# Layer 0 message weighting on VectorE: one two-harmonic product with the harmonics in PSUM and one addition, instead of one product and four scalar passes

## The reference

```
xs_e, xv_e = x[src][:, :64], x[src][:, 64:].reshape(E, 32, 3)      # rows of the source nodes
es, ev = edge_feat[:, 0], edge_feat[:, 1:4]                        # the four harmonics of an edge
out_s = (xs_e*es @ W_ss / 8 + einsum('eud,ed,uo->eo', xv_e, ev, W_vv) * ISQ3 / sqrt(32)) * ISQ2
out_v = (einsum('eu,ed,uv->evd', xs_e, ev, W_sv) * ISQ3 / 8 + einsum('eud,e,uv->evd', xv_e, es, W_vs) * ISQ3 / sqrt(32)) * ISQ2
messages = concat([out_s, out_v]) * sigmoid(edge_scalars @ W_rad.T + b_rad)
agg = segment_sum(messages, dst)
```

## Time and profile before

| | us |
|---|---|
| median of 3 runs | 4404.54 (4403.96 to 4408.41) |
| the profiled execution | 4403.6 |
| its span in the trace | 4401.8 |
| VectorE busy | 3921.4 (89%) |
| TensorE busy | 4086.9 (93%) |
| GpSimd busy | 3161.6 (72%) |
| ScalarE busy | 2637.0 (60%) |

### The profile page before, as it was taken

The page is one execution under the profiler, slowest core; times in us unless marked ns, Lnnn a source line. Parts: engine busy times, 40 slices in busy tenths (PEclk is TensorE's granted clock), DMA queues, the critical chain, the costliest instruction groups (busy, mean ns, idle before and its releaser), DMA issues.

```text
span 4401.8 us, 60923 instructions
## 1 busy us (share of the span) xinstructions
PE 4086.9 (93%) x12412; PEld 2529.0 (57%) x12413; DVE 3921.4 (89%) x8792; ACT 2637.0 (60%) x8195; POOL 3161.6 (72%) x3268
## 2 busy tenths in 40 slices
PE   6988899988999988999889999999999999999997
PEld 3666666666666666666655555555555555555555
DVE  4999999999999999999768888888888888888887
ACT  2666666666666666666556666666666666666664
POOL 3777777777777777777457777777777777777771
PEclk8566655565555566555789999999999999999998
DMA  8666666666666666666333333333333333333331
GB/s 261 191 192 193 191 193 193 192 194 193 191 194 193 193 193 191 192 194 192 114 93 101 103 101 101 103 102 100 103 101 103 102 100 103 101 102 103 100 101 53
DMA packets 245761, 640.14 MB, mean 145 GB/s; under 512 B 57085, under 2 KB 95407, under 8 KB 245627
## 3 DMA queue, kind: packets, MB, share of 16 engines
q0 software_dynamic: 181152, 556.66, 45.9%
q1 hardware_dynamic: 64576, 83.11, 6.0%
HBM read 618.66 MB, written 20.88 MB: 145 GB/s over the span
## 4 chain that ended last, share of the span: by engine, by line
DVE 42%; PE 19%; issue 12%; ACT 9%; DMA 8%; POOL 5%; DVEq 5%; ACTq 0%; POOLq 0%; SPq 0%
DVE work L686 13%; PE ps L985 11%; ACT work L477 9%; DVE work L667 8%; DVE onehot L727 7%; DMA work<-table,srcs 6%; POOL work L380 5%; DVE work L660 3%; PE ps L978 3%; DVE acc L735 2%; DVE work L675 2%; PE ps L972 2%; DVEq L792 1%; DVE arena L735 1%; DVEq L727 1%
## 5 line engine op out<-in xcount | busy, mean ns | idle before, releaser
L380 POOL DMA_INDIRECT work<-table,srcs x1596 | 1550.1, 971 | 486.5 <-issue 461.2
L380 POOL DMA_INDIRECT arena<-table,srcs x1596 | 1540.2, 965 | 494.7 <-issue 468.2
L985 PE MATMUL ps<-work,onehot 128*128 128x384 f32 x3608 | 1275.0, 499 | 39.2 <-DVE onehot L727 35.8
L477 ACT ACTIVATE work<-work,harm 128x96 f32<-128x96 f32 (+1 forms) x3224 | 1071.4, 415 | 268.2 <-DMA work<-table,srcs 254.2
L985 PE MATMUL ps<-arena,onehot 128*128 128x161 f32 x3608 | 1015.0, 457 | 208.0 <-DVE arena L692 181.0
L985 PEld LDWEIGHTS ps<-arena,onehot 128*128 128x128 f32 x3608 | 866.8, 303 | 524.0 <-issue 454.3
L477 ACT ACTIVATE work<-arena,harm 128x160 f32<-128x160 f32 (+1 forms) x3224 | 984.9, 389 | 152.5 <-DMA arena<-table,srcs 105.8
L985 PEld LDWEIGHTS ps<-work,onehot 128*128 128x128 f32 x3608 | 654.1, 190 | 549.9 <-issue 124.7
L965 PE MATMUL ps<-wrad,escal 49*128 49x320 f32 x1612 | 890.2, 697 | 0.0
L727 DVE SCALAR_TENSOR_TENSOR onehot<-ps,bases,dst_sh 128x512 f32<-128x512 f32 x902 | 673.0, 746 | 14.3 <-DVE acc L735 7.3
L686 DVE TENSOR_REDUCE work<-work 128x256 f32<-128x768 f32 (+1 forms) x806 | 654.6, 853 | 0.1
(11 more groups left out here) (130 smaller groups left out, 2430.6 us busy)
## 6 DMA issues: line engine op xcount, KB each, us to landing
escal<-in_escal SPq DMA_DIRECT2D x404, 98.0 KB
arena<-table,srcs POOLq DMA_INDIRECT x1596, 3.5
work<-table,srcs POOLq DMA_INDIRECT x1596, 2.7
table<-work SPq DMA_DIRECT2D x49, 224.0 KB, 4.5
dst_sh<-in_dst_sh SPq DMA_DIRECT2D x52, 160.0 KB, 3.0
table<-work SPq DMA_DIRECT2D x7, 784.0 KB, 4.0
acc<-in_xd SPq DMA_DIRECT2D x1, 3920.0 KB, 28.1
arena<-in_xd SPq DMA_DIRECT2D x7, 560.0 KB, 4.2
```

The lines of the kernel that those rows point to most:

```text
L380: pool.indirect_dma_start(out=rows[:, j, t, :], out_offset=None, in_=table, in_offset=bass.IndirectOffsetOnAxis(ap=of[:, j, t:t + 1], axis ...
L477: last = nc.scalar.activation(u[:, t, to:to + c1 - c0], r[:, t, c0:c1], ACT.Copy, scale=harm[:, j, at:at + 1])
L985: last = mm(bank(to)[:, 0:(MSG0, MSG1)[l]], onehot[:, b, t, :], m[:, j % 2, t, :], start=t == 0, stop=t == TPS - 1)
```

## The change

In layer 0, VectorE now weights with harmonics 1 and 2 in one `tensor_tensor` of 4 x 2 x 96 elements per partition, out of `rows0` into columns 384 to 576 of `weighted0` (which grows from 544 to 576 columns per row), and adds the second half onto columns 128 to 224 with one `tensor_tensor` of 4 x 96. The harmonics of this product come from `harm0`, 64 columns in PSUM bank 7, into which VectorE copies those of all four supertiles at the start of each round, straight from `dst_sh`. The addition waits for the product (`s_wone`), the product of a round's first supertile for the copy (`s_harmp`); `messages0` waits for the addition (`s_headed`). `s_wone`, which lets POOL refill the slot, is now signalled by the product. The waits for `s_add` inside the four passes are gone, and that for `s_agg` stands behind the addition. The columns of the table are put in another order, with the same sizes of ACT's and TensorE's instructions.

```diff
-PARTS0 = 544
+PARTS0 = 576
...
+        harm0 = hps[:, 0:4 * TPS * SLOTS].rearrange("p (j c) -> p j c", j=SLOTS)
...
-                weight(u, r, 3, 96, 256, 128, j % PAIR).then_inc(s_whead, 1)
-                weight(u, r, 0, 256, 352, 288).then_inc(s_wtd[0], 1)
+                weight(u, r, 3, 192, 352, 128, j % PAIR).then_inc(s_whead, 1)
+                weight(u, r, 0, 352, 448, 288).then_inc(s_wtd[0], 1)
...
+            def of_round(i, j, c):
+
+                return dst_sh[:, :, :].rearrange("p (q j) c -> p q j c", j=SLOTS)[:, bass.ds(i % (2 * CHUNK), 1), j, c].rearrange("p o j c -> p (o j) c")
+
...
                 if l == 0:
+                    if j == 0:
+                        nc.vector.tensor_copy(harm0, of_round(i, slice(0, SLOTS), slice(TPS, 5 * TPS)).bitcast(f32)).then_inc(s_harmp[0], 1)
                     dve.wait_ge(s_whead, s + 1)
                     u, r = weighted0[:, j % DEEP0, :, :], rows0[:, j, :, :]
-                    nc.vector.tensor_tensor(u[:, :, 384:480], r[:, :, 352:448], by(1), ALU.mult)
-                    for t in range(TPS):
-                        if t == 1:
-                            dve.wait_ge(s_add[0], s + 1)
-                        if t == TPS - 1 and not opens:
-                            dve.wait_ge(s_agg[0], s + 1)
-                        to = u[:, t, 128:224]
-                        last = nc.vector.scalar_tensor_tensor(to, r[:, t, 0:96], harm[:, j, 4 * t + 2:4 * t + 3], to,
-                                                              ALU.mult, ALU.add)
+                    if j == 0:
+                        dve.wait_ge(s_harmp[0], i + 1)
+                    nc.vector.tensor_tensor(u[:, :, 384:576].rearrange("p t (k c) -> p t k c", k=2),
+                                            r[:, :, 0:192].rearrange("p t (k c) -> p t k c", k=2),
+                                            bc(harm0[:, j, :].rearrange("p (t k) -> p t k", k=4)[:, :, 1:3], 3, [P, TPS, 2, 96]),
+                                            ALU.mult).then_inc(s_wone[0], 1)
+                    dve.wait_ge(s_wone[0], s + 1)
+                    nc.vector.tensor_tensor(u[:, :, 128:224], u[:, :, 128:224], u[:, :, 480:576], ALU.add).then_inc(s_headed, 1)
+                    if not opens:
+                        dve.wait_ge(s_agg[0], s + 1)
...
-                dve.wait_ge(s_wone[0], s + 1)
+                dve.wait_ge(s_headed, s + 1)
...
-                mm(p[:, 32:128], x1[:, of_tile], w0b[:], start=False, stop=True).then_inc(s_tmm, 1)
+                mm(p[:, 128:224], x1[:, of_tile], w0b[:], start=False, stop=True).then_inc(s_tmm, 1)
```

More of the change, by code:

```diff
@@ L197, in mk_gnn_resnorm_d2_gnn_r8_694f30_kernel @@
         s_wtd = [sem(f"rows_weighted{l}") for l in range(2)]
+        s_harmp = [sem(f"harmonics_in_psum{l}") for l in range(2)]
         s_whead = sem("scalar_parts_weighted")
         s_wone = [sem(f"rows_weighted_by_dve{l}") for l in range(2)]
+        s_headed = sem("third_harmonic_added")
         s_part = [sem(f"message_part{l}") for l in range(2)]
@@ L220, in mk_gnn_resnorm_d2_gnn_r8_694f30_kernel @@
         I8, I32, I96 = MS ** -0.5, MV ** -0.5, (MS + MV) ** -0.5
-        SCALED0 = [(w0a[0:64, 128:192], I8 * ISQ2), (w0a[0:64, 0:128], I8 * ISQ3 * ISQ2), (w0a[0:64, 192:448], I8 * ISQ3 * ISQ2),
+        SCALED0 = [(w0a[0:64, 224:288], I8 * ISQ2), (w0a[0:64, 0:224], I8 * ISQ3 * ISQ2), (w0a[0:64, 288:448], I8 * ISQ3 * ISQ2),
                    (w0a[64:128, :], I32 * ISQ3 * ISQ2), (w0b[:], I32 * ISQ3 * ISQ2)]
@@ L675, in weight_by_one @@
                     last = nc.vector.tensor_tensor(u[:, :, 448:544], r[:, :, 128:224], by(2), ALU.mult)
-                last.then_inc(s_wone[l], 1)
+                    last.then_inc(s_wone[1], 1)
             def messages0(s, j):
                 u, m, c = weighted0[:, j % DEEP0, :, :], msg0[:, j % 2, :, :], rad[j % 2]
-                dve.wait_ge(s_wone[0], s + 1)
+                dve.wait_ge(s_headed, s + 1)
                 def summed(to, at, k):
@@ L723, in select @@
             def select(i, j, b, window):
-                of_round = dst_sh[:, :, :].rearrange("p (q j) c -> p q j c", j=SLOTS)
-                dst = of_round[:, bass.ds(i % (2 * CHUNK), 1), j, 0:TPS].rearrange("p o t -> p (o t)")
+                dst = of_round(i, slice(j, j + 1), slice(0, TPS)).rearrange("p o t -> p (o t)")
                 return nc.vector.scalar_tensor_tensor(onehot[:, b, :, :], bc(numbers(FIRST + b), 1, [P, TPS, P]),
@@ L1217 @@
         "attr": placed(NODES_PAD, 1, (0, 0, attr)).reshape(NODE_TILES, P).T,
-        "w0a": placed(P, ROW0, (0, 0, wsv), (0, 128, wss), (64, 192, wvs), (96, 224, wvs),
-                      (64, 256, wvv), (0, 320, wsv), (0, 352, wsv), (96, 384, wvv)),
+        "w0a": placed(P, ROW0, (0, 0, wsv), (96, 32, wvv), (0, 96, wsv), (0, 224, wss), (64, 288, wvs), (96, 320, wvs),
+                      (64, 352, wvv), (0, 416, wsv)),
         "w0b": placed(P, 96, (0, 0, wvv), (0, 64, wvs)),
```

## The result

| | before | changed |
|---|---|---|
| median, us | 4405.78 (4 runs, 4403.96 to 4408.41) | 4465.73 (4 runs, 4465.51 to 4470.42) |
| profiled span, us | 4401.8 | 4463.8 |
| changed / before | | 1.0136, 95% interval 1.0124 to 1.0148 |

The changed kernel is 1.4% slower, 59.9 us by the medians; the forecast was 64 us. In the comparisons further down the kernel before lay between 4406 and 4408 us in the median; each ratio is against the runs beside it.

What follows compares the result with a forecast made beforehand. VectorE and GpSimd were taken to bound layer 0 together, within 0.3%. Product and addition +24, copies +41, given back 1: +64 us on 4404.5, so 4468 us, range 4418 to 4498.

Steps and rivals of the forecast that it cites:

- The step from the chain of starts: Layer 0: VectorE (5.064 us a supertile) and GpSimd (5.08) both set the pace, so work VectorE gains is paid in full.
- The total: Whole kernel: 24 + 41 - 1 = +64 us, giving 4468 us, 1.4% slower.
- The pair: Layer 0, new product and addition replacing old product and four passes: 1.46 against 1.40 us a supertile, +24 us.
- the hold: VectorE, layer 0: the addition, waiting for the product just before it, starts 0.04 us after that product's end.
- The copy: VectorE, start of each layer 0 round: 64 columns into PSUM, 0.41 us in 100 rounds, +41 us (0 to +70).
- The extra address work: VectorE's sequencer at a round's start: the copy's source address depends on the round, one more piece of work, 0.15 us.
- The wait at the layer's end: End of layer 0: VectorE no longer waits there; of 1.97 us about 1 is given back.
- Rival A: Layer 0: the addition isn't held, 1.33 against 1.40 us, saving 24 us; with the copies 4420 us; chance 0.08.
- B: Layer 0: each wait for the instruction before costs 0.15 us, adding 44 and 4 us: 4516 us; chance 0.08.
- C: Layer 0: the copy vanishes in the round's idle time, the rest as forecast, +23 us: 4428 us; chance 0.07.
- Rival D: Layer 0: VectorE falls below 5.064 us, GpSimd bounds with quicker gathers, faster: 4390 us, 4374 at most; chance 0.07.

Runs made afterwards that it cites:

- the best kernel: Changed kernel with addition behind the sums, copy a round ahead, product split with the added part in PSUM, one-hot matrix between reductions and multiplication: 4371.91 us, ratio 0.9922.

## Why the prediction was right

The step from the chain of starts held: the two engines stood level, VectorE's side grew, and it was paid in full. By its own points:

- The total came closer than its terms. Layer 0 was forecast at +64 and grew by 58.2; the pair came out 4 over its forecast and the copy 10 under, and about 4 us of the difference in span lie outside the layer. That the medians differ by 59.9 is in part luck.
- The pair: +0.06 forecast, +0.07 measured (24 and 28 us). The product 0.95 us, the hold 0.03 to 0.04, both as taken from layer 1 and from the reductions. The addition was 0.01 dearer than L660, 564 ns in the mean against its median of 553.
- The copy: its 0.22 us (0.228 measured) and its hold were right, but the term was too large, +0.41 forecast and +0.31 measured, 41 and 31 us. The extra address work, put at 0.15, showed as 0.05: the sequencer's work of 0.13 us that carries the copy's address also holds the wait that had taken 0.06 by itself, so only the difference was new. The wait at the layer's end gave back 2.0 us where about 1 was put.
- Rival A fell by the moved addition, B by the 0.03 between product and addition, C by the copy alone. GpSimd waited (its idle time rose by 67 us), as forecast; VectorE did not wait for ACT in mid-layer.
- Rival D had its condition right (VectorE under 5.064 us) and its prize nearly right in size (30 us at most; the best kernel got 36 by the medians, of which GpSimd's pace, 5.08 to 5.00 us, is 403 x 0.08 = 32). What it lacked is that a lighter VectorE alone doesn't reach it: with instructions of two SBUF inputs left in each supertile GpSimd stayed at 0.964 to 0.973 us a gather in three kernels. It named the sources of the delay but not that the cost of one grows with the square of its length.

Left open is why TensorE, at a mean granted clock of 0.58 in layer 0 of the changed kernel and 0.59 in the fastest one, bounded neither, the latter at 5.0 us a supertile; no run changed its work.

## What to carry to other kernels

Cost a chain of short VectorE instructions by the distances of their starts: the five old ones had 1.8 us of durations against 1.5 in the new two, and were the quicker ones, since a dependent neighbour costs 0.118 us each time and an independent instruction put between them gives it back. Before making the busiest engine lighter, look for a second one whose gaps never change: GpSimd at 75% busy with nearly all gaps at 0.30 us was as much a bound as VectorE at 94%. And where such a GpSimd issues gathers, it pays to keep one of the two inputs of long VectorE instructions in PSUM, or the instructions short: cutting the one of 768 elements in two took the longest delay from 0.78 to under 0.4 us and cost VectorE 0.07 us.

## What the runs showed of the hardware

A gather on GpSimd (0.946 us when undisturbed) that starts beside a VectorE `tensor_tensor` with both inputs in SBUF lasts until about that instruction's end and then its own rest: up to 1.72 us beside one of 768 elements, up to 1.33 beside one of 384, and where such instructions follow each other it gets in between them. Of the 184 gathers of the changed kernel that start beside its product, with one input in PSUM, none lasts over 0.96 us. With no instruction of two SBUF inputs in the layer the mean of 1583 gathers is 0.945. The Trainium skill (SBUF — State Buffer, section "Who interferes with whom") says that a VectorE instruction with two SBUF inputs contends with a GpSimd instruction that reads SBUF, and infers that making a transfer's descriptors isn't touched by it. The first half agrees with the runs here; of the indirect gathers, which take their row numbers from SBUF, the second half doesn't hold.
